# Attention stage of a two-layer decoder: where VectorE normalises h, and where it scales y for the experts

## The reference, cut to what matters

```python
x = x + _L0_attn_ref(_layernorm(x), ...)            # first stage
x = x + _L0_xattn_ref(_layernorm(x), ctx, ctx)      # second stage: the change is here
x = x + _L0_ffn_ref(_layernorm(x), ...)             # third stage: it reads y = rms(layernorm(x))
...
# _L0_xattn_ref: 32 query heads of 8, 8 key heads of 8, 128 queries, 128 keys
scores = jnp.einsum('bkgsd,bktd->bkgst', qh, kh) / scale
weights = jax.nn.softmax(scores, axis=-1)
out = jnp.einsum('bkgst,bktd->bkgsd', weights, vh)
```

## Time and profile before

| What | Value |
|---|---|
| Times of the kernel before, median of 3 | 1420.72 us (1419.54 to 1421.12) |
| Profiled execution, its own time | 1405.85 us |
| Its span, first to last instruction | 1404.0 us |
| Busy share: PE, DVE, ACT, POOL | 87%, 68%, 54%, 43% |
| Mean granted TensorE clock | 0.947 of full |
| Second stage | from 137.8 to about 295.0 us |

### The profile page before, as it was taken

One profiled execution on the slowest core, in us unless ns is written; L12 is line 12 of the kernel. 1 busy time (PEld: TensorE's weight loads), 2 busy tenths in 40 slices (PEclk: granted clock), 3 DMA queues, 4 the chain that ended last, 5 costly groups with the idle time before them and its releaser, 6 DMA issues. The chain is left out here.

```text
span 1404.0 us, 24766 instructions
## 1 busy us (share of the span) xinstructions
PE 1216.4 (87%) x7679; PEld 943.2 (67%) x7726; DVE 960.2 (68%) x1863; ACT 760.1 (54%) x1757; POOL 603.5 (43%) x737
## 2 busy tenths in 40 slices
PE   6895899989989983499989999999977888869998
PEld 5673444467879873377777777777754555648887
DVE  5999899836755358877877778777854666633443
ACT  5433577753555453566666666666643555533332
POOL 2000556352164553766676666666644333320000
PEclk9997999969999996699999999999997999989999
DMA  9001000010035313200000000000000000000000
GB/s 330 2 1 55 14 16 17 9 61 1 16 106 150 93 55 154 109 1 1 1 0 0 0 0 0 0 0 0 1 1 6 3 3 3 3 1 1 16 15 31
DMA packets 27422, 44.74 MB, mean 32 GB/s; under 512 B 5648, under 2 KB 22160, under 8 KB 25936
## 3 DMA queue, kind: packets, MB, share of 16 engines
q1 hardware_dynamic: 23888, 34.31, 7.1%
q0 software_dynamic: 3456, 9.44, 2.6%
HBM read 32.21 MB, written 9.44 MB: 30 GB/s over the span
## 5 line engine op out<-in xcount | busy, mean ns | idle before, releaser
L2312 ACT ACTIVATE wi_weights<-wi_psum,wi_bias,wi_scale 128x128 f32<-128x128 f32 x256 | 113.7, 454 | 120.1 <-DVE wi_bias L2432 120.1
L2087 POOL TENSOR_TENSOR wi_straight<-wi_straight,wi_crossed 128x512 f32<-128x512 f32 x80 | 103.0, 1287 | 10.9 <-DVE wi_crossed L2418 10.8
L975 DVE TENSOR_REDUCE gq_least<-gq_psum 128x4 f32<-128x512 f32 x128 | 84.6, 686 | 13.8 <-PE gq_psum L858 12.1
L2075 POOL TENSOR_TENSOR wi_scratch<-wi_sums,wi_eps 128x4 f32<-128x4 f32 x80 | 33.7, 421 | 131.0 <-DVE wi_sums L2391 129.6
L2076 POOL TENSOR_TENSOR wi_scale<-wi_scratch,minus_half 128x4 f32<-128x4 f32 x80 | 84.6, 1057 | 6.3
L2202 PE MATMUL wi_psum<-wi_k_t,wi_q_t 128*128 128x128 f32 x512 | 68.3, 277 | 20.7 <-ACT wi_q_t L2303 19.5
L937 ACT ACTIVATE gq_weights_t<-gq_psum 128x512 f32<-128x512 f32 x128 | 67.7, 601 | 23.4 <-PE gq_psum L878 23.2
L2153 PEld LDWEIGHTS wi_psum<-const,wi_straight 128*128 128x128 f32 x320 | 39.1, 142 | 55.9 <-issue 37.4
L2852 DVE TENSOR_REDUCE cr_top<-cr_psum 128x4 f32<-128x512 f32 x64 | 43.7, 682 | 46.4 <-PE cr_psum L2667 46.4
L2423 DVE TENSOR_REDUCE wi_top<-wi_psum 128x4 f32<-128x512 f32 x64 | 43.9, 686 | 45.9 <-PE wi_psum L2202 45.9
L2211 PE MATMUL wi_psum<-wi_weights_t,wi_values 128*128 128x512 f32 x128 | 68.1, 613 | 2.8 <-DVE wi_weights_t L2439 1.3
(11 more groups left out here) (415 smaller groups left out, 3818.8 us busy)
## 6 DMA issues: line engine op xcount, KB each, us to landing
slot_y<-ex_s_out SPq DMA_DIRECT2D x20, 256.0 KB, 2.5
x<-in_x_dram SPq DMA_DIRECT2D x4, 512.0 KB, 7.9
gate<-in_gate_dram SPq DMA_DIRECT2D x2, 1024.0 KB, 6.4
up<-in_up_dram SPq DMA_DIRECT2D x2, 1024.0 KB, 8.4
down<-in_down_dram SPq DMA_DIRECT2D x2, 1024.0 KB, 10.5
egu<-in_egu_dram SPq DMA_DIRECT2D x1, 2048.0 KB, 15.9
gq_keys_diagonal<-gq_key_parts SPq DMA_DIRECT2D x64, 32.0 KB, 1.9
wo<-in_wo_dram SPq DMA_DIRECT2D x1, 2048.0 KB, 8.8
```

The costliest lines, as they stand in the source:

```text
L975: dve.tensor_reduce(least[:, n // 2 % 2, n % 2, j, :], ps[:, j % 2, :].rearrange("p (v t) -> p v t", t=P), AX.X, ALU.min).then_inc(topped, 1)
L2087: added_up = pool.tensor_tensor(straight[:, at], straight[:, at], crossed[:, at], ALU.add)
L2312: act.activation(weights[:, g % 2, j, :], ps[:, SC + g % 2, j * P:j * P + P], ACT.Exp, bias=bias[:, g % 2, j:j + 1], scale=scale[:, g, j:j ...
```

## The change

DVE's `normalise` moves from between the second and the third minimum to behind `split_least`, at the end of the same even half. POOL's `split_h`, which waits for it, moves with it. The twelve L1028 (now L1029) move from the end of half 29 to the end of half 28. `ffn_norm_scale` on POOL moves from behind the loop over t into its last round, ahead of `add(13)`. The six `normalise_ffn` move from half 32 to half 30 (blocks 0 to 3) and half 31 (blocks 4 and 5). Nothing is computed otherwise, and no instruction is added or removed.

```diff
@@ POOL, loop over t
             for t in range(NB):
+                if t == NB - 1:
+                    pool.wait_ge(aggregated_ffn, NB - GB)
+                    ffn_norm_scale(pool, own, net, scratch, scratch2, slice(0, NB - GB)).then_inc(rstd_ffn, 1)
                 if t >= 2:
                     add(t - 2)
...
                 own.again()
-            pool.wait_ge(aggregated_ffn, NB - GB)
-            ffn_norm_scale(pool, own, net, scratch, scratch2, slice(0, NB - GB)).then_inc(rstd_ffn, 1)
             add(NB - 2)
             add(NB - 1)
@@ DVE, loop over n
                 for j in range(4):
                     if n + LEAD < HALVES:
                         minimum(n + LEAD, j)
-                    if j == 1 and n >= 0 and n % 2 == 0 and n // 2 + 3 < NB:
-                        if n == 2:
-                            dve.wait_ge(rstd_ready, 1)
-                        normalise(n // 2 + 3)
                     if j == 2 and n >= 5 and n % 2 and n // 2 < NB:
                         measure(n // 2 - 2)
                 if n % 2 == 0 and n + LEAD < HALVES:
                     split_least((n + LEAD) // 2)
-                if n == HALVES - 3:
+                if n >= 0 and n % 2 == 0 and n // 2 + 3 < NB:
+                    if n == 2:
+                        dve.wait_ge(rstd_ready, 1)
+                    normalise(n // 2 + 3)
+                if n == HALVES - 4:
                     for b in range(NB - GB):
                         dve.bn_aggr(net.mean_var[:, b, :], net.stats[:, b, :]).then_inc(aggregated_ffn, 1)
-                if n == HALVES:
-                    dve.wait_ge(rstd_ffn, 1)
-                    for b in range(6):
-                        normalise_ffn(dve, net, b)
+                for b in {HALVES - 2: range(4), HALVES - 1: range(4, 6)}.get(n, ()):
+                    if b == 0:
+                        dve.wait_ge(rstd_ffn, 1)
+                    normalise_ffn(dve, net, b)
```

## The result

The kernel after takes 1429.38 us in the median of its runs (1423.58 to 1432.07), the kernel before beside them 1419.54 (1414.26 to 1421.12). The ratio is 1.0077, with a 95% interval of 1.0057 to 1.0096: some 0.8% slower, where 0.5% faster was forecast. The profiled execution of after has an own time of 1423.58 us. Its page hides the reason, as the one of before did: span, busy time of each engine (share, instructions).

What follows compares the result with a forecast made beforehand. Two engines, PE and DVE, were nearly full in the second stage, with PE waiting for DVE's L983, stalled beside POOL. 4.9 + 1.1 - 0.15 + 1.2 = 7.0 us off the median 1420.72 gave 1413.7 us, range 1408 to 1418.

Steps and rivals of the forecast that it cites:

- Both cost nothing: In the loop, POOL's later key split with its transfers and the later transposes of h were taken to cost 0.
- 6.9 in all: POOL's work from the end of `normalise` (splits, keys, values, fold, add), to fit the 7.6 us before the next L983.
- Even halves longer: Sign of being wrong: even halves of the second stage longer than 3.97 us.
- Odd halves, 4.9 us: Blocks 4 to 15: without L983's stall, twelve odd halves fall from 4.86 to 4.45 us, 0.41 each.
- half 1, 1.1 us: The first place of the stall, with a wait of 1.13 us, gains 1.1 us (0.9 to 1.3).
- Normalise exposed: Rival: `normalise` ahead of `divide` uses up 0.17 us of slack; 0.07 us gained per odd half, 1417.8 us; chance 0.12.
- Divide blocked by POOL's splits: Rival: L999 stalls beside POOL's splits of h in thirteen odd halves; 25 us lost, 1439 us; chance 0.05.
- Aggregation sooner, -0.15 us: Twelve L1028 ahead of a divide start `attend` about 0.75 us later; 0.15 us (0.1 to 0.75) stays lost.
- Scales and y sooner, 1.2 us: End of the second stage: earlier scales and y writes gain 1.2 us (0.4 to 1.9), collisions with adds included.
- full block: `tensor_scalar` writes of y and POOL's two adds fully block each other at stage end; 0.4 us gain left.
- the clock stays up: Rival: behind the second stage, a shorter PE gap keeps the clock from falling; priced at 9 us, 1404.7; chance 0.13.
- 14.87 us: Amount by which the median of before, 1420.72 us, lies above its profiled execution, carried over to the forecast.

Runs made afterwards that it cites:

- e1: The kernel after with POOL's add moved directly behind the splits of h in rounds 1 to 12; median 1411.42 us, ratio to before 0.9932 to 0.9967.
- e4: The kernel after with four halves of `gq_out` in place of two, POOL's order unchanged; median 1410.51 us, ratio to before 0.9918 to 0.9957.
- e2: The kernel after with only the move of `normalise` kept, aggregation, scales and y back as in before; median 1430.65 us, ratio to before 1.0037 to 1.0091.
- e7: e4 with the twelve aggregations behind the divide of half 29 and y written as three, two and one; median 1409.48 us, ratio to before 0.9924 to 0.9972.
- after again: The kernel after, unchanged, profiled once more; half 0 to half 28 took 134.70 us.
- e6: The kernel before with only POOL's add moved directly behind the splits of h in rounds 1 to 12; median 1418.47 us, ratio to before 0.9985 to 1.0020.
- e3: The kernel after with `normalise` put back, aggregation, scales and y still moved; median 1419.28 us, ratio to before 0.9978 to 1.0025.
- e5: The kernel after without POOL's eight folds of third-stage weights; median 1415.02 us, ratio to before 0.9951 to 0.9998.
- e8: The kernel before, unchanged, profiled once more; own time 1421.78 us.

## Why the prediction was wrong

**The step that failed** is the price of moving `normalise`. The prediction follows POOL's later round to the keys and to h ("Both cost nothing") and puts the third thing that waits for that round, the add that frees `gq_out`, at nothing without naming it. The runs showed 15.9 us lost there and some 3.6 in the clock beside it, against 6.2 won. The reckoning of POOL's round was at hand. I counted "6.9 in all" from the end of `normalise` for the heaviest round, and that was right: in the round with 1.13 in place of 2 us of fold it took 5.86 (192.18 to 198.04). I held it against "7.6", the time until the next L983. But L983 was not the first that needs POOL's round to be over. The divide of the even half does, 3.94 us behind `normalise` (196.12, where L997 ends). 5.86 - 3.94 = 1.92, the wait of 2.03. The same subtraction gives 0.8 without a fold and 2.8 with two experts' halves, against 0.9 and 2.87 measured. The lengths for it stood in the profile before. "Even halves longer" was among my signs of being wrong, but no rival stood behind it, and a slower kernel had a chance of 0.04.

**Why it was missed.** I listed what POOL's splits feed (transposes, keys) and what disturbs them. I did not list what waits for everything else in POOL's round, the add above all, since no wait of L999 for L804 showed. In rounds with the 1.13 us fold the edge was met by 0.87 to 0.90 us. An edge of that kind has no row in the view of waits; it stands in the code, and in the timeline as two rows close together. In the two rounds with the longest fold, the very ones that I had counted 6.9 us for, the rows were 0.10 apart, with nothing left to move into. And POOL's idle 3.62 us ahead of its split is no room for the add: it stands behind the add, and does not move its due time.

**Odd halves, 4.9 us, and half 1, 1.1 us: right.** 4.45 us in all twelve of e1 and e4, and in eleven of after (half 19 is 4.91, with a half-clock stretch reaching into it); 1.29 for half 1, at the upper end. That it is "more than the wait of 0.33" held too.

**Normalise exposed: did not occur.** `attend` starts 1.77 us behind its half's L877 in e1 (1.82 behind L875 in after) without a wait; the 0.17 us of slack was enough.

**Divide blocked by POOL's splits: did not occur.** L1000 is 0.29 us beside L792 in every half. The rule of the Trainium skill cited in the prediction (SBUF — State Buffer, Who interferes with whom) held here. But the divide was delayed by POOL after all, by a semaphore in the *even* half, not by contention in the odd. I had priced the right victim and the wrong mechanism; the mark that I set, a loss when the divide ends over 0.7 us late, was passed in the even halves, where I had not applied it.

**Aggregation sooner, -0.15 us.** `attend` did start 0.72 us late, and half 29 grew by 0.25. But half 30 fell from 2.73 to 2.50, so by half 31 nothing of it was left (5.61 us for the two, before and after); the term was 0, just outside its 0.1 to 0.75.

**Scales and y sooner, 1.2 us.** With aggregation, 1.05 was forecast; e4, free of the missed wait, has 1.14 and after 0.58. The second missed edge, `add(13)` behind 6 us of scales, takes 0.56. Four y beside an add took 1.77 us in e4 and 1.37 without one in after, so a collision costs 0.4, below the 0.7 that I allowed; but both adds met writes of y and not one (the two y of the second took 1.02 in e4, for two times 0.34 alone). The full block behind the prediction's lower end did not show: when the four y began, the add had 0.66 us to go, and 0.4 was lost.

**The clock behind the stage.** PE's gap fell from 4.15 us to 3.36 (3.01 in e4). The clock fell at this place in all eleven profiles, so "the clock stays up" did not occur. How long it stayed down differs: in the 35 us from the gap on it was at half for 27.3 us in before (twice) and e2, 23.9 in e7 and after again, 20.5 in e6, 17.1 in after, e3, e4 and e5, 13.7 in e1. From the third stage's start to VectorE's first reading of its logits it took 20.3 us in the first five of these, 17.2 in after, e3, e5 and e6, 16.9 in e4 and 14.1 in e1. So it varies by 3 us between two executions of after. Of the five profiles with a gap of 3.5 to 4.2 us four have 20.3, of the six with 3.0 to 3.4 us one has. A shorter gap may thus be worth some 3 us, as the rival's "a part of it" has it; but e3, with the gap at 3.36, has the median of before. The part is neither shown nor refuted.

**The base.** Carrying the 14.87 us over was sound: e8 shows that they belong to that execution.

## What to carry to other kernels

Before an engine's work is moved later, list every instruction whose semaphore that engine raises in the whole round, buffers given back among them, and for each the time until its waiter is due; the smallest of these is what the move may cost, and an edge that is met has no row in the view of waits. In the timeline, look at the heaviest round, where the waiter starts closest behind what it waits for. Idle time of an engine is room only for the work that stands behind it in the list. If a move fails on such an edge, one more buffer or one step of reordering on the delayed engine can return the whole gain: here 8 to 9 us under before instead of 10 over.

## What the runs showed of the hardware

A wait can cost more than itself. In a stage that runs at full clock without them, waits of PE of 1.7 to 2.6 us had 3.4 us at half of it beside them, three times in one execution and twice in each of two others. A slowed half was 1.5 us longer than its twin (7.21 against 5.67), and part of that came back in the next; over the stage 3.6 us were left over for three, and 1.8 for two (134.70 - 123.15 - 9.7). In the loop of e5, with waits of 0.6 us, and in that of before, e1, e3, e4 and e7, where `attend` waits nowhere, the clock stayed up. Which of the waits gets such a stretch, the runs don't tell.

Not every two-input instruction of POOL stops one of DVE. Beside L793, which reads and writes 128x512, the split of extremes took 1.14 us. Before the loop, in the kernel before, the same instruction ran inside the 2.27 us of POOL's power at its normal 0.21:

```profile
149.23 2.27 POOL L198 TENSOR_TENSOR rstd<-gq_scratch,minus_half 128x12 f32<-128x12 f32 x1
150.19 0.21 DVE L983 TENSOR_TENSOR gq_least_parts<-gq_least,ones 128x32 fp32r<-128x32 f32 x1
```

And one profiled execution can be 14 us off in a part that the change doesn't touch: from the first reading of the third stage's logits to the residual sum it took 213 us once and 221 to 227 in ten others.
